# Twelve-head attention: the row maximum moves into a spare row of the second score product

## What is computed

```python
qkv = (xn @ qkv_w.T + qkv_b).reshape(Bx, Nx, 3, H, hd).transpose(2, 0, 3, 1, 4)
q, k, v = (qkv[0], qkv[1], qkv[2])
attn = jax.nn.softmax(jnp.einsum('bhqd,bhkd->bhqk', q, k) * scale, axis=-1)
o = jnp.einsum('bhqk,bhkd->bqhd', attn, v).reshape(Bx, Nx, C)
x = x + (o @ proj_w.T + proj_b)
```

## Time and profile before

| what | us |
|---|---|
| time, median of 3 runs (2574.82 to 2578.39) | 2577.34 |
| the profiled execution: its time | 2573.1 |
| its span, first to last instruction | 2571.3 |
| PE busy in the span | 2368.5 (92%) |
| DVE busy | 1657.7 (64%) |
| ACT busy | 1156.4 (45%) |
| POOL busy | 1042.0 (41%) |

### The profile page before, as it was taken

How to read it: one execution, slowest core, us unless ns; L and a number is a source line. 1 busy time by engine, 2 the same in 40 slices (tenths; PEclk the granted TensorE clock), 3 DMA queues, 4 the chain that set the end, 5 groups by cost and what they waited for, 6 DMA issues and landing times. The chain is left out here.

```text
span 2571.3 us, 63751 instructions
## 1 busy us (share of the span) xinstructions
PE 2368.5 (92%) x19496; PEld 1829.1 (71%) x19496; DVE 1657.7 (64%) x4146; ACT 1156.4 (45%) x2240; POOL 1042.0 (41%) x1196
## 2 busy tenths in 40 slices
...
PEclk7669999999999999899999999999999998999998
...
GB/s 135 142 61 111 32 36 35 49 40 32 36 33 44 47 32 32 141 68 102 115 98 106 119 117 104 97 116 91 101 110 106 87 148 183 232 225 225 239 218 132
...
## 3 DMA queue, kind: packets, MB, share of 16 engines
...
HBM read 217.71 MB, written 58.33 MB: 107 GB/s over the span
## 5 line engine op out<-in xcount | busy, mean ns | idle before, releaser
L1356 DVE TENSOR_REDUCE MX<-PS 108x2 f32<-108x648 f32 x576 | 455.9, 824 | 46.3 <-PE PS L1778 41.6
L1051 ACT ACTIVATE pool<-PS 108x648 f32<-108x648 f32 x576 | 386.8, 713 | 214.0 <-PE PS L1801 185.7
L899 POOL DMA_INDIRECT out<-big,tokn x192 | 304.2, 1584 | 415.7 <-DVE big L1506 234.0
L1657 PE MATMUL PS<-WB,big 128*128 128x192 f32 x2304 | 405.8, 331 | 2.5 <-ACT big L1080 2.5
L1080 ACT ACTIVATE big<-PS,WF 128x256 f32<-128x256 f32 x576 | 241.9, 473 | 350.3 <-PE PS L1657 348.3
L1657 PEld LDWEIGHTS PS<-WB,big 128*128 128x128 f32 x2304 | 374.8, 191 | 27.8 <-issue 19.1
L1657 PE MATMUL PS<-XE,WF 128*128 128x256 f16 x2880 | 358.9, 276 | 22.8 <-DMA WF<-w1p 15.0
L1657 PEld LDWEIGHTS PS<-XE,WF 128*128 128x128 f16 x2880 | 274.5, 99 | 75.9 <-issue 16.9
L876 POOL DMA_INDIRECT xbuf<-XR,DST x192 | 190.6, 993 | 238.4 <-issue 154.1
L1506 DVE SCALAR_TENSOR_TENSOR big<-PS,grow,GB 128x192 f32<-128x192 f32 x192 | 71.2, 413 | 271.6 <-POOL GB L887 152.7
L1812 PE MATMUL PS<-pool,Vp 108*32 108x324 f32 x2304 | 216.2, 518 | 0.0
...
## 6 DMA issues: line engine op xcount, KB each, us to landing
...
```

The source lines that it names most:

```text
L899: nc.gpsimd.indirect_dma_start(rows_out, bass.IndirectOffsetOnAxis(ap=tokn[:, i, s_:s_ + 1], axis=0), Yt[:, i, s_, :], None, bounds_check= ...
L1051: nc.scalar.activation(Pr[:, at:at + 2, :], pair(("st", p))[0:TP, :, 0:T], ACT.Exp, scale=SCALE2).then_inc(S["ex"], 1)
L1356: nc.vector.tensor_reduce(MX[:, qt, g, 64 * jj:64 * jj + 64:32], pair(("s", p))[0:TP, :, 0:T], AX.X, ALU.max).then_inc(S["mx"], 1)
L1657: last = nc.tensor.matmul(out_ap, lhsT, rhs, start=(i == 0), stop=(i == len(products) - 1))
```

## The change

In words: `KL` gets 32768 in row 16 of each head's 32, which `query_bias` adds to the bias of k there. `qm` is now q rounded in the *lower* sixteen rows and zero in the upper ones, and it is no longer only an intermediate: `mx` writes its maxima to column 16 of each 32 (and not to column 0), and `nm` adds -max/32768 into that row of `qm`. The second product of `st` is `KL` by `qm`, which carries the maximum with it; the third product, `big16` and `NM` are gone. Products of the two remainders fall away with this.

Who adds the row to `qm` depends on the list. In ATTEND turns PE does it: `mt` first multiplies `qm` by a unit matrix into the bank (one product, 324 columns) and then, in place of three transposes, adds three fp32 products of `MX` with a unit matrix times -1/32768; `nm` stays a copy on ACT, now into `qm`. In BOTH and LAST turns `mt` keeps its transposes and `nm` moves to DVE, as one instruction that reads PSUM and `qm` and writes `qm`. The lists and bank tables of ATTEND, BOTH and LAST are written anew.

```diff
             def nm(b, g):
                 act.wait_ge(S["mt"], due("mt", b, g + 1))
-                act.wait_ge(S["st"], due("st", b - 1, 6 * g + 6))
-                nc.scalar.activation(NM[:, g, :], bank(("mt", g))[:, 0:T], ACT.Copy, scale=-1.0 / BIG).then_inc(S["nm"], 1)
+                nc.scalar.activation(qm[:, g, :], bank(("mt", g))[:, 0:T], ACT.Copy).then_inc(S["nm"], 1)
...
+            def nm(b, g):
+                dve.wait_ge(S["mt"], due("mt", b, g + 1))
+                nc.vector.scalar_tensor_tensor(qm[:, g, :], bank(("mt", g))[:, 0:T], -1.0 / BIG, qm[:, g, :],
+                                               ALU.mult, ALU.add).then_inc(S["nm"], 1)
...
-                nc.vector.tensor_scalar(qmb[:, :], qkb[:, 0:3], mq, None, ALU.mult).then_inc(bias_ready, 1)
+                nc.vector.tensor_scalar(qmb[:, 0:3], qkb[:, 0:3], mq, None, ALU.mult)
+                nc.vector.tensor_scalar(qmb[:, 3:6], qkb[:, 3:6], top, None, ALU.add).then_inc(bias_ready, 1)
...
+                if turn.plan is ATTEND:
+                    nc.tensor.matmul(ps[:, 0:T], id16[:, :], qm[:, g, :], start=True, stop=False)
                 for qt in range(NT):
-                    last = nc.tensor.transpose(ps[:, TP * qt:TP * qt + TP], MX[:, qt, g, :], ident[0:TP, 0:TP])
+                    at = ps[:, TP * qt:TP * qt + TP]
+                    if turn.plan is ATTEND:
+                        last = nc.tensor.matmul(at, MX[:, qt, g, :], cst[0:TP, C_DOWN:C_DOWN + TP],
+                                                start=False, stop=qt == NT - 1)
+                    else:
+                        last = nc.tensor.transpose(at, MX[:, qt, g, :], ident[0:TP, 0:TP])
...
-                for n, (left, right) in enumerate(((KH[:, g, k], QA[:, g, :]), (KL[:, g, k], QA[:, g, :]),
-                                                   (big16[:, :], NM[:, g, :]))):
+                for n, (left, right) in enumerate(((KH[:, g, k], QA[:, g, :]), (KL[:, g, k], qm[:, g, :]))):
...
 BOTH_STEPS = [
-    ("mx", 10), ("mt", 0), ("mx", 11), ("W1", 1, 1), ("nm", 0), ("rs", 0), ("rm", 1), ("s", 12), ("ge", 1, 1),
+    ("ge", 1, 0), ("W1", 1, 1), ("v1e",), ("mx", 13), ("mt", 0), ("nm", 0), ("s", 14), ("ge", 1, 1), ("s", 15),
```

More of the change, by code:

```diff
@@ L61 @@
 C_TOK = C_LE + E * E
-C_N = C_TOK + NT
+C_TOP = C_TOK + NT
+C_DOWN = C_TOP + 1
+C_N = C_DOWN + TP
 XIN = 6 * 16
@@ L98 @@
 ATTEND_STEPS = [
[15 rows of a table removed]
[14 rows of a table added]
+    ("qkl", 1), ("qkh", 2), ("gt2",), ("no", 2), ("scat",), ("qkl", 2),
 ]
 ATTEND_BANKS = {
[10 rows of a table removed]
[10 rows of a table added]
 }
 BOTH_STEPS = [
[21 rows of a table removed]
[20 rows of a table added]
+    ("qkh", 2), ("qkl", 2), ("scat",),
 ]
 BOTH_BANKS = {
[1 row of a table removed]
[1 row of a table added]
     ("W1", 0, 1): (6,), ("s", 2): (4, 5), ("s", 3): (2, 3), ("s", 4): (0, 1), ("W1", 0, 2): (6,), ("s", 5): (4, 5),
[11 rows of a table removed]
[11 rows of a table added]
 }
@@ L364, in build_program @@
         qkb = sb("qkb", [128, 6], F32)
-        qmb = sb("qmb", [128, 3], F32)
+        qmb = sb("qmb", [128, 6], F32)
         cst = sb("cst", [128, C_N], F32)
         ident = cst[:, C_ID:C_ID + 128]
-        m64, mq = (cst[:, c:c + 1] for c in (C_M64, C_MQ))
+        m64, mq, top = (cst[:, c:c + 1] for c in (C_M64, C_MQ, C_TOP))
         rev = cst[0:TP, C_REV:C_REV + NT * E].rearrange("p (t e) -> p t e", t=NT)
@@ L779, in _ @@
             nc.gpsimd.memset(MX[:, :, :, :], 0.0).then_inc(pad_set, 1)
-            nc.gpsimd.memset(big16[:, :], BIG).then_inc(pad_set, 1)
             nc.gpsimd.memset(zrow[:, :, :], 0.0).then_inc(zero_set, 1)
@@ L1094, in run @@
                     if kind == "preps":
-                        act.wait_ge(pad_set, 4)
+                        act.wait_ge(pad_set, 3)
                         prep("qkv")
```

20 lines of the change are left out of this document (11 added, 9 removed), and 168 rows, old and new, of tables (ATTEND_BANKS, ATTEND_STEPS, BOTH_BANKS, BOTH_STEPS).

## The result

| kernel | median, us | lowest to highest |
|---|---|---|
| before | 2576.1 | 2562.3 to 2578.4 |
| changed | 2617.4 | 2608.0 to 2626.7 |

The change makes the kernel slower: the time is 1.0181 of that before, with a 95% interval of 1.0152 to 1.0209. Forecast were 2543 us, faster, and a range of 2510 to 2574.

What follows compares the result with a forecast made beforehand. PE was taken to bound BOTH; in ATTEND, PE and DVE wait for each other. 13 BOTH turns gave -32.5 us, two other turns -5, 17 ATTEND turns +3: together -34.5, a median of 2543 us, range 2510 to 2574.

Steps and rivals of the forecast that it cites:

- Part 1: BOTH turns: dropping the third product of each `st` and regrouping the list takes 2.5 us off a turn.
- the regrouping: New BOTH list: one run of `st` less, worth 0.43 us, and one run of `s` less, worth 0.28.
- DVE's `nm`: Rival for BOTH: `nm` on DVE is late three times a turn, 16 us in all, 2559 us; chance 0.10.
- The tail: Second filling turn and LAST: 2.5 us less each, 5 us together.
- Part 2: Who adds the row: an ATTEND `mt` costs PE 0.46 us more, 1.4 a turn; DVE's `nm` elsewhere is taken as free.
- Part 3: Order in ATTEND: waits mended and waits made nearly cancel, +0.05 us in a turn, between -1.5 and +1.6.
- The slower rival: ATTEND: PE stands still ahead of `s1` and the clock falls, 3.7 us a turn, 63 us, 2603 us; chance 0.10.
- More products keep the clock up: ATTEND: 21 products in place of 9 transposes spare a low-clock piece, 27 us off, 2516 us; chance 0.04.
- The third product was covered in ATTEND: ATTEND: removing it only turns into waiting, so 1.25 us a turn don't come, 21 us more, 2564 us; chance 0.11.
- the BOTH term: 13 BOTH turns at -2.5 us each, -32.5 us; its bounds are -20 to -42.

Runs made afterwards that it cites:

- pool_fixed: Changed kernel with ATTEND's list and banks of before; in BOTH `gb` 0 behind `n0`, `xh` behind `xm`, `xl` behind `is1`; 0.9947 of before.
- fixed_new: Changed kernel, new ATTEND list kept, with three BOTH steps moved: `gb` 0 behind `n0`, `xh` behind `xm`, `xl` behind `is1`; 0.9985 of before.
- old_both: Changed kernel with the lists and banks of BOTH and LAST from before; products and ATTEND stay new; 1.0070 of before.
- pe_rows: Changed kernel with all lists of before, and PE adding the row in every turn, `nm` a copy on ACT; 0.9987 of before.
- again: The changed kernel itself, measured once more, unaltered; 1.0202 of before, 2633.3 us.
- dve_rows: Changed kernel with all lists of before, transposes in every `mt` and `nm` on DVE in every turn; 1.0289 of before.
- old_lists: Changed kernel with all lists and banks of before, so the new products alone; 1.0042 of before, 2598.6 us.
- third_kept: Changed kernel with all lists of before, and ATTEND keeping the third product, transposes and ACT's `nm` into `NM`; 1.0035 of before.
- fixed_kept: `pool_fixed` with ATTEND keeping the third product, its transposes and ACT's `nm` into `NM`; 0.9943 of before.
- gb_later: Changed kernel with one step moved in the BOTH list: `gb` 0 behind `n0` in place of ahead of `is0`; 1.0415 of before, 2696.9 us.
- xh_earlier: Changed kernel with two steps moved in the BOTH list: `xh` behind `xm` and `xl` behind `is1`; 1.0267 of before, 2656.0 us.

## Why the prediction was wrong

**What bounds the kernel** was read rightly: in BOTH, what TensorE doesn't do comes off the time, if nothing new makes it wait.

**Part 1, BOTH.** The work went as forecast: 69.34 to 67.55 us at full clock, -1.8 against -2.5 taken and -1.5 to -3.2 as bounds. The time of a turn, forecast at 69.3, is 69.5 in `pool_fixed` (833.6 / 12) and 72.6 in the changed kernel. That 69.5 is so near is partly luck. At full clock a turn went from 70.20 to 69.15 us, -1.05 and not -2.5: the regrouping brought less than its 0.7, and TensorE stands still for 1.45 us in place of 0.86. The rest of the gain came from the clock, for which the sum had no term: eleven of the twelve turns before have a low piece of 3.4 us or more, and five of twelve in `pool_fixed`.

**The step that failed** is in the same part: "It all counts, since PE is busy for 99% here." That holds for an order that stays. The cost of the new order in BOTH was looked for on PE and on DVE alone; POOL's queue, past which `scat`, `ad` 2, `xl` and `gb` 0 were moved, was never written down. It could have been. With `xl` behind the last products of a turn, its 1.4 us, the two adds (3.8 with their pauses) and the six scatters (7.7) must follow each other from there, and end 9.8 us into the next turn in place of 5.1; `gb` 0 adds 1.5 and `is0` 1.2, which makes 12.6, where DVE is free for `n0` at 9.8. That is 2.8 us in a turn and takes back the 2.5, before the clock. It is a rival of the kind that the prediction asked for, a wait in place of the one removed, but its only candidate for it was DVE's `nm`.

The sign of being wrong that the prediction named for BOTH, a gain of less than 1.5 us in a turn, came: the turn lost 0.8.

**The tail**, all behind the twelve turns, was forecast at -5 (the last BOTH turn and LAST). It takes 12 us more than before in the changed kernel and 3 us more in `fixed_new`, so that most of this follows from the same queue; why the -5 didn't come wasn't traced further. With 9 us more in ATTEND, this is also why `pool_fixed`, with 28 us off its BOTH turns, is only some 14 us faster than before; no kernel here reaches 2543.

**Part 2.** An `mt` in ATTEND takes 0.89 us, not 0.74: six passes at 0.125 us, where 0.10 was taken between rows at 0.093 and 0.115. (The three transposes of an `mt` in BOTH take 0.37 to 0.40 us in the changed kernel, not 0.28, so that the difference is 0.5, near the 0.46 of the sum.) By the Trainium skill (TensorE: Matmul & The Clock Gate, LDWEIGHTS) the passes would be bound by their loads at 0.64 us; the measured 0.75 is above that too. TensorE's work in an ATTEND turn came out as forecast all the same: 51.1 us at a clock of 0.94, and 51.08 in a turn of before at 0.94 (502.20 to 556.50).

**DVE's `nm`** (0.10). In the new BOTH list it is covered, as worked out: TensorE has no wait for `qm` in the turn at 1481.74. In the old list it isn't: the waits that come with it eat most of the 1.5 us of a turn (`old_both` against `pe_rows`). So here the new order did what the sum said.

**Part 3, ATTEND.** Forecast +0.2 us in a turn, 54.2. Found are 54.61 in the changed kernel, and 55.2 (`fixed_new`) and 56.1 (`again`) as means. The waits hardly grew: TensorE is idle for 3.5 us in a turn, 3.4 before, and `s1` waits 0.22 us, as in the earlier trace rows. Turns of before with as much low clock (6.8 us) take 54.2 to 54.4 us, so that 0.3 us in a turn are the change's own, near the forecast. The rest is the clock: every turn of the changed kernel has 6.8 us of it, while of the fifteen before five had 3.4, nine 6.8 and one 10.2.

**The slower rival** (0.10) had the sign and 2603 us, near the 2617 found, but not the mechanism: PE doesn't stand still ahead of `s1`, and `v1` back in its old place made the turns longer. **More products keep the clock up** (0.04) didn't come: with the 21 products ATTEND's clock is 0.94, and it was 0.95. Whether transposes count less for the clock, as the Trainium skill says (TensorE: Matmul & The Clock Gate, Part 4), isn't settled by these runs. `dve_rows`, with the transposes back, has 0.87 where `old_lists` has 0.95, but its `nm` is on DVE as well; `third_kept`, with transposes too, has 0.94. **The third product was covered in ATTEND** (0.11) is half right. From `fixed_kept` to `pool_fixed` TensorE is busy for 0.9 us less in a turn and stands still for 1.05 us more, so what is taken from it does turn into waiting under the old ATTEND list. But by the rival the turn would grow by the whole 1.4 us of the longer `mt`, and it grows by 0.14.

**The range** ended at 2574, short of the slower case; the bounds of the BOTH term held for the work of TensorE only, and no bound stood for what the order does on POOL.

**What stays open.** Why ATTEND turns of the same code settle at 54.61 us in one kernel and at 61.44 in another. The list of BOTH also orders the two filling turns ahead of the ATTEND turns, and the first ATTEND turn of `gb_later` takes 60.6 us where that of the changed kernel takes 56.0. That a slow first turn is kept up doesn't explain it, though: in `old_both` it takes 60.2 us and all fifteen behind it 54.61, while `again` starts with 54.5 and then has turns of 56 to 60. Open too is what held the readers of `emb` and of the first `W1` in `xh_earlier` and `gb_later`.

## What to carry to other kernels

When a change reorders a turn, write down every engine's queue at the places where the bound engine waits now, the lightly loaded engines above all: a GpSimd at 41% held up a kernel in which TensorE was at 92%, because six scatters of 1.3 us stood ahead of a 1 us step on the chain. Price work removed from the bound engine and the new order as two terms, and try them apart: here the products with the old lists gave nothing, the new lists with the old products lost 4%, and new products with the new BOTH list, three steps put back and ATTEND's list left as it was, gained 0.5 to 0.7%. Undo a suspected cost in full before dropping the suspicion, since each of the two moves, made alone, gave a slower kernel. And compare turns at the same clock: over half of what a BOTH turn gained in `pool_fixed` is a low piece that came less often.

## What the runs showed of the chip

**A share of low clock can repeat from turn to turn.** ATTEND turns of the same code took 54.61 us (clock 0.94) or 61.44 us (0.83), and each value repeated to 0.03 us over nine turns and more, in `gb_later` from 604 us to the end of ATTEND; the other engines' busy time was the same to 0.3 us, and TensorE waited 0.7 us more in the long turns. Over fifteen turns the difference is up to 99 us (`gb_later` against the changed kernel), more than any part of the sum.

**One length of a turn, by two ways.** An ATTEND turn takes 54.61 us in the changed kernel with 3.5 us in which TensorE stands still and a clock of 0.94, and 54.6 us in the settled turns of `old_lists`, under the old ATTEND list, with 5.7 us and 0.97. So that two variants have the same turn doesn't show that their products cost the same.

**In one place the clock falls behind a wait of TensorE.** In BOTH turns of the changed kernel it fell in the wait of 2.83 us or at most 2 us behind it, in five turns of twelve; a turn takes 71.5 us without a fall and 75.5 with 10.2 us of it. Not every such wait brings one: the same code does both. Nor is a wait needed: before, it fell some 54 us into eleven of twelve BOTH turns, in each of which TensorE stands still for 0.9 us in all.

**Less work was once slower by more than its waits.** `dve_rows` took products from TensorE in ATTEND and made turns of 57 to 64 us, at clocks of 0.91 to 0.76. TensorE stands still for 6.0 us in these turns, and for 5.7 in those of 54.6 us in `old_lists`.
